# Low-rank factors in both halves of the partitions, multiplied in two rounded passes of 128 and 64 rows

## The chip, the core and the metric

One Trainium2 chip; the program runs on one of its cores. The metric is the device time in microseconds. Each time is one execution; of several the median is given.

## What is computed

A transformer block with adaptive layer norm. Only what bears on the change is shown: the second half is a mixture of eight experts, and the first two experts of the reference have low-rank additions to each of their three weight matrices.

```python
weights = _router_weights(x, Wr, temperature)
gate = jnp.einsum('btd,edf->ebtf', x, Wg)
up = jnp.einsum('btd,edf->ebtf', x, Wu)
gate = gate.at[:NL].add(jnp.einsum('btd,edr,erf->ebtf', x, Ga, Gb))
up = up.at[:NL].add(jnp.einsum('btd,edr,erf->ebtf', x, Ua, Ub))
mid = jax.nn.silu(gate) * up
out = jnp.einsum('ebtf,efd->ebtd', mid, Wd)
out = out.at[:NL].add(jnp.einsum('ebtf,efr,erd->ebtd', mid[:NL], Da, Db))
return jnp.einsum('bte,ebtd->btd', weights, out)
```

`NL` is 2, the rank `R` is 64, `D` and `F` are 256. The attention before it has 8 batches of 256 rows, 16 query heads and 4 key heads of 128.

## The kernel before

All instructions are written by hand for each engine, with semaphores between them; no scheduler moves anything. The order of the source is the order on the engine.

Attention runs in 64 slots, one for two heads of one batch: scores, tanh and exponential, the product with the values, the output projection, and beside these the projections of the next batch. Then come 32 tiles, each one expert on 512 rows (`TILES`, index `m`). A tile has two steps `up(g)`, each 24 matmuls of 512 columns into `ps_g` and `ps_u`, and two steps `down(d)`, each 12 matmuls of 256 columns. The first four tiles are spread over the last slots; from `m = NEXT = 4` on there is a loop over `m` on each engine.

Nearly every product is made of three passes over rounded data: an operand is stored as a rounded part (`hi`, type float32r) and the rest (`lo`), and `three` multiplies hi by hi, hi by lo and lo by hi. ScalarE rounds (`we_hi`, L1027), GpSimd subtracts (`we_lo`, L1660). Transposes, the router's logits, the product with the values (L663) and the low-rank products take plain float32.

Low-rank weights: rather than adding a product to every output, the kernel multiplies the two factors once, adds the 256x256 result to the expert's weight matrix while that still lies unrounded in `raw_e`, and lets the ordinary rounding follow. `low_rank(i)` (L754) has six calls, three matrices of each of two experts. Each multiplies two blocks of `lowA` by `lowB` into one PSUM bank, `ps_y` or `ps_turn` in turn. `fold(i)` on VectorE (L1331) adds the bank to `raw_e`. The two experts stand third and fourth in the kernel's order. The calls stand at the ends of four steps of the loop over the tiles, `LOW_STEPS`: two calls with m = 5, one with 6, one with 8, two with 9.

```python
LOW_STEPS = {NEXT + 1: [0, 1], NEXT + 2: [2], NEXT + 4: [3], NEXT + 5: [4, 5]}
...
                for k in range(KT):
                    mm = pe.matmul((ps_y[:], ps_turn[:, 0, :])[i % 2][:, k * F:(k + 1) * F], lowA[:, e, m3, k * P:(k + 1) * P],
                                   lowB[:, e, m3, :], start=(k == 0), stop=True, skip_group_check=True)
```

`lowA` and `lowB` take 64 partitions (the rank) by 2 x 3 x 256 elements. SP issues their loads (L521, L522) once the last output projection is done (`y_ready`), since they lie where the output weights were; behind them on the same queue stand the gate rows (`gates_b`, L523) and the remaining experts (`raw_e`, L505).

In step m = 4 ScalarE does the gate activations (`gate_of`, L1035), the normalised rows of the last batch, the rounding of `mid`, and `modulate2` for the last batch; in step m = 5 it rounds this batch (`h2_head`, L1011) between the two gate activations, and VectorE makes its low part `h2_lo` (L1323), which tile m = 6 is the first to read. GpSimd has `inv_std2` for the last batch, and then the low parts of the experts, from m = 6 on.

Of the kernel before, what the change touches and what calls it, by code (L numbers as in the profile page):

```python
# [13 lines left out]
P = 128  # L14
# [209 lines left out]
def build(nc, a, out):  # L224
# [16 lines left out]
    def sem(name):  # L241
        return ctx.enter_context(nc.semaphore(name))

    with ctx:
# [98 lines left out]
        r_eq = [place(f"r_eq{n}", [P, 4, NE, NE], F32, offset + 1024) for n, offset in enumerate((raw_at + 10240, h2f_at, probs_at + BLOCK))]  # L343
        part = place("part", [P, 2, TT, E], F32, k_at[1] + 4 * 4 * E)
        part_last = place("part_last", [P, 4, E], F32, k_at[1] + 4 * 4 * E + 4 * 2 * TT * E)
        lowA = place("lowA", [R, NL, 3, E], F32, wo_at)
        lowB = place("lowB", [R, NL, 3, E], F32, wo_at + 4 * NL * 3 * E)
        gates_b = place("gates_b", [P, B, E], F32, wo_at + 4 * H * E)

        raw_o = raw_e[:].rearrange("p a m f -> p (a m f)").rearrange("p (r k n) -> p r k n", r=RAW_RING, k=KT)  # L350
# [27 lines left out]
        cs_in = sem("cs_in")  # L378
        qks_in = sem("qks_in")
        low_in = sem("low_in")  # L380
        out_done = sem("out_done")
        silu_c = sem("silu_c")
        mod_cols = sem("mod_cols")
# [90 lines left out]
        def _(sp):  # L474
# [43 lines left out]
            sp.wait_ge(we_split, 1)  # L518
            expert(2)
            sp.wait_ge(y_ready, B)  # L520
            sp.dma_start(lowA[:], a["lowA"]).then_inc(low_in, 16)  # L521
            sp.dma_start(lowB[:], a["lowB"]).then_inc(low_in, 16)  # L522
            sp.dma_start(gates_b[:], gates_dram[:, E:2 * E].unsqueeze(0).broadcast_to([P, B, E])).then_inc(gates_b_in, 16)  # L523
            for e in range(3, NE):
                sp.wait_ge(we_split, 3 * (e - 1) - 2)
# [11 lines left out]
        def _(pe):  # L537
# [216 lines left out]
            def low_rank(i):  # L754

                e, m3 = divmod(i, 3)
                if i == 0:
                    pe.wait_ge(low_in, 32)
                    pe.wait_ge(x_updated, B)
                elif i == 1:  # L760
                    bank_free(len(TURN_LIST), 0)
                else:
                    pe.wait_ge(we_added, i - 1)
                for k in range(KT):
                    mm = pe.matmul((ps_y[:], ps_turn[:, 0, :])[i % 2][:, k * F:(k + 1) * F], lowA[:, e, m3, k * P:(k + 1) * P],
                                   lowB[:, e, m3, :], start=(k == 0), stop=True, skip_group_check=True)
                mm.then_inc(low_ready, 1)

            def slot(s):
# [85 lines left out]
        def _(act):  # L855
# [183 lines left out]
            def mid_head(g):  # L1039
# [3 lines left out]
                    act.wait_ge(down_ready, 2 * m - 2)  # L1043
                act.activation(mid_hi[:, m % 2, f, :], mid[:, f, :], ACT.Copy, scale=0.5 if g < SMOOTH else 1.0).then_inc(mid_hi_done, 1)  # L1044

            def route(g, stage):
                if stage == 0:
                    act.wait_ge(router, STEPS * g + 2)
                    act.activation(r_b[:], r_a[:], ACT.Exp, scale=-1.0).then_inc(router_act, 1)
                else:  # L1050
                    act.wait_ge(router, STEPS * g + 8)
                    act.activation(r_w[:], r_c[:], ACT.Exp, scale=-1.0 / 0.1).then_inc(router_act, 1)
                    act.activation(r_fb[:], r_c[:], ACT.Exp, scale=-1.0 / 0.3).then_inc(router_act, 1)
# [78 lines left out]
            for m in range(NEXT, len(TILES)):  # L1132
                gate_of(2 * m)
                if m in LATE_ROUTE_EXP:
                    route(LATE, LATE_ROUTE_EXP[m])
                if m == NEXT:
                    second_rows(B - 1)
                if m == NEXT + 1:
                    h2_head(B - 1)
                gate_of(2 * m + 1)  # L1140
                mid_head(2 * m)
                mid_head(2 * m + 1)
                if m == NEXT:
                    modulate2(B - 1)
                for e, m3 in EXPERT_STEPS.get(m, ()):
                    split_e(e, m3)

# [423 lines left out]
        def _(pool):  # L1571
# [149 lines left out]


            inv_std2(B - 1)
            for m in range(NEXT, len(TILES)):
                for e, m3 in EXPERT_STEPS.get(m, ()):
                    split_e(e, m3)
# [64 lines left out]
```

## Time and profile before

| what | value |
|---|---|
| median of 3 runs | 808.05 us (807.27 to 809.63) |
| the profiled execution | 808.01 us |
| its span | 806.3 us |
| TensorE busy | 795.3 us, 5116 matmul records |
| TensorE weight loads busy | 710.1 us |
| VectorE, ScalarE, GpSimd busy | 507.5, 462.2, 395.0 us |
| granted TensorE clock | full in all 40 slices |
| DMA | 21.53 MB, mean 27 GB/s |

The span is the time from the first to the last instruction that the profile has; the execution's own time has some 1.7 us more around it. A weight load is a record of its own (PEld) and runs beside matmuls (PE). The ends of matmuls are modelled, and overlap; what can be relied on is the distance from start to start. An unrounded float32 matmul is recorded as two.

### The profile page before, as it was taken

What the parts mean: (1) busy time and instruction counts of PE and PEld (TensorE: products, weight loads), DVE (VectorE), ACT (ScalarE), POOL (GpSimd) and SP (SyncE); (2) the same over time, 40 slices, a digit from 0 to 9 for tenths busy, and PEclk for the clock granted to TensorE, in tenths of its full rate; (3) what the DMA queues carried; (4) which work ended last, traced back from release to release, by engine and by line L of the source; (5) the groups of instructions that cost most, each with busy time, mean ns of one, the idle gap of its engine ahead of it and who ended that gap; (6) DMA issues with size and microseconds to landing.
All of it is one profiled execution on the core that took longest, in us unless ns stands there. A gap on an engine that the chain in (4) does not pass through costs nothing.

```text
span 806.3 us, 14755 instructions
## 1 busy us (share of the span) xinstructions
PE 795.3 (99%) x5116; PEld 710.1 (88%) x5116; DVE 507.5 (63%) x1074; ACT 462.2 (57%) x1255; POOL 395.0 (49%) x543
## 2 busy tenths in 40 slices
PE   9899999999999999999999999999999999999997
PEld 8688898999999999999999999899888888888887
DVE  5677676476476566557557658667785454454575
ACT  5777686677577677667767776643343232332322
POOL 3777587486576667567567656120011010110493
PEclk9999999999999999999999999999999999999999
DMA  9200010000000000000000000203010110100002
GB/s 333 103 28 2 1 61 1 1 8 2 0 8 2 1 7 2 2 2 6 1 1 8 1 2 2 79 1 94 38 40 2 40 40 1 40 0 1 1 1 105
DMA packets 8170, 21.53 MB, mean 27 GB/s; under 512 B 1561, under 2 KB 4249, under 8 KB 7969
## 3 DMA queue, kind: packets, MB, share of 16 engines
q1 hardware_dynamic: 7520, 20.51, 7.5%
q8 instruction: 42, 0.69, 0.4%
q14 instruction: 32, 0.25, 0.1%
q10 hardware_dynamic: 576, 0.08, 0.1%
HBM read 18.48 MB, written 2.11 MB: 26 GB/s over the span
## 4 chain that ended last, share of the span: by engine, by line
PE 93%; DVE 2%; POOL 1%; ACT 1%; issue 1%; DMA 1%; ACTq 0%; DVEq 0%; POOLq 0%
PE ps_o L663 14%; PE ps_proj L540 9%; PE ps_proj L542 9%; PE ps_proj L541 9%; PE ps_s L540 7%; PE ps_s L541 7%; PE ps_s L542 7%; PE ps_turn L592 4%; PE ps_y L540 4%; PE ps_y L541 4%; PE ps_y L542 4%; PE ps_turn L610 3%; PE ps_turn L540 2%; PE ps_turn L541 2%; PE ps_turn L542 2%; PE ps_o L542 2%
## 5 line engine op out<-in xcount | busy, mean ns | idle before, releaser
L663 PE MATMUL ps_o<-vaug,probs 128*128 128x129 f32 x1024 | 135.3, 275 | 1.6 <-POOL probs L1654 0.9
L663 PEld LDWEIGHTS ps_o<-vaug,probs 128*128 128x128 f32 x1024 | 129.1, 191 | 8.0 <-POOL probs L1654 1.4
L984 ACT ACTIVATE ps_s<-ps_s,knorm 128x512 f32<-128x512 f32 x128 | 79.1, 657 | 95.7 <-PE ps_s L542 95.5
L1267 DVE RECIPROCAL rden<-ps_o 128x2 f32<-128x2 f32 x128 | 21.8, 170 | 154.0 <-PE ps_o L663 153.9
L1660 POOL TENSOR_TENSOR we_lo<-raw_e,we_hi 128x512 fp32r<-128x512 f32 x22 | 28.4, 1316 | 182.3 <-ACT we_hi L1027 182.3
L1237 DVE TENSOR_TENSOR prod<-ps_proj,cs 128x1024 f32<-128x1024 f32 x76 | 92.5, 1217 | 10.9 <-ACT sq L927 10.9
L1605 POOL TENSOR_TENSOR root<-ssq,powers 128x4 f32<-128x4 f32 x76 | 77.7, 1023 | 27.6 <-ACT sq L927 27.6
L927 ACT ACTIVATE sq<-ps_proj 128x128 f32<-128x128 f32 x304 | 79.9, 278 | 18.2 <-PE ps_proj L542 15.2
L1621 POOL TENSOR_TENSOR prod<-prod 128x512 f32<-128x512 f32 x62 | 80.0, 1290 | 9.9 <-DVE prod L1237 9.9
L540 PE MATMUL ps_proj<-w_hi,h_hi 128*128 128x512 f32 x192 | 83.1, 433 | 0.9 <-DVE w_lo L1180 0.5
L1652 POOL TENSOR_SCALAR_AFFINE_SELECT probs<-probs 128x256 f32<-128x256 f32 x64 | 26.3, 410 | 106.1 <-ACT probs L992 105.8
L540 PE MATMUL ps_y<-wo_hi,oT_hi 128*128 128x256 f32 x256 | 75.8, 296 | 0.0
L542 PE MATMUL ps_proj<-w_hi,h_lo 128*128 128x512 f32 x192 | 75.7, 394 | 0.0
L541 PE MATMUL ps_proj<-w_lo,h_hi 128*128 128x512 f32 x192 | 75.4, 393 | 0.0
L1628 POOL TENSOR_TENSOR rows<-prod,rnorm 128x512 f32<-128x512 f32 x62 | 66.7, 1075 | 13.2 <-issue 4.7
L542 PE MATMUL ps_y<-wo_hi,oT_lo 128*128 128x256 f32 x256 | 71.4, 279 | 0.0
L541 PE MATMUL ps_y<-wo_lo,oT_hi 128*128 128x256 f32 x256 | 71.4, 279 | 0.0
L1044 ACT ACTIVATE mid_hi<-mid 128x512 fp32r<-128x512 f32 x64 | 40.2, 629 | 47.9 <-DVE mid L1352 26.0
L992 ACT ACTIVATE probs<-ps_s 128x1024 f32<-128x1024 f32 x64 | 66.2, 1035 | 0.0
L927 ACT ACTIVATION_READ_ACCUMULATOR sq<-ps_proj 128x1 f32 x304 | 63.4, 209 | 0.0
L1271 DVE TENSOR_TENSOR o_rows<-ps_o,rden 128x256 f32<-128x256 f32 x128 | 54.3, 424 | 4.4
L540 PE MATMUL ps_proj<-h_hi,we_hi 128*128 128x512 f32 x140 | 55.6, 397 | 0.0
(212 smaller groups left out, 2178.1 us busy)
## 6 DMA issues: line engine op xcount, KB each, us to landing
raw_e<-in_we SPq DMA_DIRECT2D x8, 768.0 KB, 4.3
raw_p<-in_wqkv SPq DMA_DIRECT2D x6, 512.0 KB, 8.1
raw_e<-in_wo SPq DMA_DIRECT2D x4, 512.0 KB, 11.6
x_all<-in_x SPq DMA_DIRECT2D x1, 1536.0 KB, 7.0
out<-acc SPq DMA_DIRECT2D x3, 512.0 KB, 2.6
x_all<-in_wmod SPq DMA_DIRECT2D x1, 1024.0 KB, 10.0
gates_a<-gate_rows_dram SPq DMA_DIRECT2D x8, 128.0 KB, 2.9
gates_b<-gate_rows_dram SPq DMA_DIRECT2D x1, 1024.0 KB, 8.0
```

What stands on the lines that cost most here:

```text
L540: pe.matmul(dst, hi, w_h, start=first, stop=False, skip_group_check=True)
L541: pe.matmul(dst, hi, w_l, start=False, stop=False, skip_group_check=True)
L542: return pe.matmul(dst, lo, w_h, start=False, stop=last, skip_group_check=True)
L663: mm = pe.matmul(ps_o[:, h * (D + 1):(h + 1) * (D + 1)], probs[:, s % 2, at:at + P], vaug[b % 2][:, k, i // 2, :], start=(h == 0 and k == ...
L927: squared = act.activation(sq[:, n % 2, h, :], ps_proj[:, u % 2, h * D:(h + 1) * D], ACT.Square, accum_out=ssq[:, n % 2, h:h + 1])
L984: act.activation(ps_s[:, t, :], ps_s[:, t, :], ACT.Tanh, scale=knorm[:, b % 2, t, i // 2:i // 2 + 1]).then_inc(tanh_done, 1)
L992: act.activation(probs[:, s % 2, :], ps_s[:].rearrange("p k n -> p (k n)"), ACT.Exp, scale=CAP).then_inc(exp_done, 1)
L1237: dve.tensor_tensor(prod[:, n % 2], src, cs[:, t].unsqueeze(2).broadcast_to([P, 2, 4, D]), ALU.mult).then_inc(rotated, 1)
L1271: dve.tensor_tensor(o_rows[:, t], o[:, :, 0:D], rden[:, t, :].unsqueeze(2).broadcast_to([P, 2, D]), ALU.mult).then_inc(o_rows_ready, 1)
L1605: pool.tensor_tensor(root[:, n % 2, :], ssq[:, n % 2, :], powers[:, 0:4], ALU.pow).then_inc(root_ready, 1)
L1621: pool.tensor_tensor(whole, whole, turned, ALU.add).then_inc(rot_sum, 1)
L1628: pool.tensor_tensor(rows[:, n % RING], prod[:, n % 2, 0], rnorm[:, n % 2, :].unsqueeze(2).broadcast_to([P, 4, D]), ALU.mult).then_inc(row ...
```

## The change

The factors are loaded twice, into partitions 0 to 63 and 64 to 127, by four DMAs. ScalarE rounds both over all 128 partitions, one expert in step m = 4 and one in step m = 5 (`low_round`). GpSimd then replaces, in partitions 64 to 127, the rounded `lowA_both` by the rest of it, and makes `lowB_lo` in partitions 0 to 63; this stands behind `inv_std2` and ahead of the experts' low parts. Each block product of `low_rank` becomes two passes over rounded data: one of 128 rows, `lowA_both` by `lowB_hi`, which gives hi by hi and lo by hi at once, and one of 64 rows, hi by lo. The product of lo by lo is left out.

```diff
-        lowA = place("lowA", [R, NL, 3, E], F32, wo_at)
-        lowB = place("lowB", [R, NL, 3, E], F32, wo_at + 4 * NL * 3 * E)
+        lowA = place("lowA", [P, NL, 3, E], F32, wo_at)
+        lowB = place("lowB", [P, NL, 3, E], F32, wo_at + 4 * NL * 3 * E)
+        lowA_both = place("lowA_both", [P, NL, 3, E], F32R, qT_at + 2 * 4 * 4 * E)
+        lowB_hi = place("lowB_hi", [P, NL, 3, E], F32R, wo_at + 4 * H * E + 4 * B * E)
+        lowB_lo = place("lowB_lo", [P, NL, 3, E], F32R, wo_at + 4 * NL * 3 * E)
...
-            sp.dma_start(lowA[:], a["lowA"]).then_inc(low_in, 16)
-            sp.dma_start(lowB[:], a["lowB"]).then_inc(low_in, 16)
+            for half in (slice(0, R), slice(R, P)):
+                sp.dma_start(lowA[half], a["lowA"]).then_inc(low_in, 16)
+                sp.dma_start(lowB[half], a["lowB"]).then_inc(low_in, 16)
...
                 if i == 0:
-                    pe.wait_ge(low_in, 32)
                     pe.wait_ge(x_updated, B)
                 elif i == 1:
                     bank_free(len(TURN_LIST), 0)
                 else:
                     pe.wait_ge(we_added, i - 1)
+                pe.wait_ge(low_split, 2 * e + 2)
                 for k in range(KT):
-                    mm = pe.matmul((ps_y[:], ps_turn[:, 0, :])[i % 2][:, k * F:(k + 1) * F], lowA[:, e, m3, k * P:(k + 1) * P],
-                                   lowB[:, e, m3, :], start=(k == 0), stop=True, skip_group_check=True)
+                    dst, at = (ps_y[:], ps_turn[:, 0, :])[i % 2][:, k * F:(k + 1) * F], slice(k * P, (k + 1) * P)
+                    pe.matmul(dst, lowA_both[:, e, m3, at], lowB_hi[:, e, m3, :], start=(k == 0), stop=False, skip_group_check=True)
+                    mm = pe.matmul(dst, lowA_both[0:R, e, m3, at], lowB_lo[0:R, e, m3, :], start=False, stop=True, skip_group_check=True)
                 mm.then_inc(low_ready, 1)
...
+            def low_round(e):
+                act.wait_ge(low_in, 64)
+                if e == 0:
+                    act.wait_ge(scores_ready, ALL)
+                    act.wait_ge(y_ready, B)
+                act.activation(lowA_both[:, e], lowA[:, e], ACT.Copy).then_inc(low_rounded, 1)
+                act.activation(lowB_hi[:, e], lowB[:, e], ACT.Copy).then_inc(low_rounded, 1)
...
                 if m == NEXT:
                     modulate2(B - 1)
+                    low_round(0)
+                if m == NEXT + 1:
+                    low_round(1)
...
             inv_std2(B - 1)
+            for e in range(NL):
+
+                pool.wait_ge(low_rounded, 2 * e + 2)
+                pool.tensor_tensor(lowA_both[R:P, e], lowA[R:P, e], lowA_both[R:P, e], ALU.subtract).then_inc(low_split, 1)
+                pool.wait_ge(low_split, 2 * e + 1)
+                pool.tensor_tensor(lowB_lo[0:R, e], lowB[0:R, e], lowB_hi[0:R, e], ALU.subtract).then_inc(low_split, 1)
+                pool.wait_ge(low_split, 2 * e + 2)
```

TensorE at the end of step m = 5, where calls 0 and 1 stand between the last pass of `down(9)` and the first of `up(12)`; before:

```order
L542 MATMUL ps_o<-we_hi_134,mid_lo 128x256
L765 MATMUL ps_y<-lowB,lowA 128x256 [waits x_updated,low_in]
L765 MATMUL ps_y<-lowB,lowA 128x256
L765 MATMUL ps_turn<-lowB,lowA 128x256 [waits logits_read]
L765 MATMUL ps_turn<-lowB,lowA 128x256
L540 MATMUL ps_s<-h_hi_128,we_hi_133 128x512 [waits mid_done,h2_split]
```

and with the change, where L774 is the pass of 128 rows and L775 the one of 64 (the size at a row's end is the output's), and L548 to L550 are the old L540 to L542:

```order
L550 MATMUL ps_o<-we_hi_134,mid_lo 128x256
L774 MATMUL ps_y<-lowB_hi,lowA_both 128x256 [waits low_split,x_updated]
L775 MATMUL ps_y<-lowB_lo,lowA_both 128x256
L774 MATMUL ps_y<-lowB_hi,lowA_both 128x256
L775 MATMUL ps_y<-lowB_lo,lowA_both 128x256
L774 MATMUL ps_turn<-lowB_hi,lowA_both 128x256 [waits low_split,logits_read]
L775 MATMUL ps_turn<-lowB_lo,lowA_both 128x256
L774 MATMUL ps_turn<-lowB_hi,lowA_both 128x256
L775 MATMUL ps_turn<-lowB_lo,lowA_both 128x256
L548 MATMUL ps_s<-h_hi_128,we_hi_133 128x512 [waits mid_done,h2_split]
```

Four matmuls became eight, and two kinds of them alternate. Nothing else on TensorE moved.

ScalarE with the change, from the end of step m = 4 to the first gate activation of step m = 6 (L1014 is `modulate2`, L1044 a gate activation, L1020 `h2_head`, L1053 the rounding of `mid`):

```order
L1014 ACTIVATE h2f_124<-ps_turn,modc 128x256
L1060 ACTIVATE lowA_both<-lowA 128x768 [waits y_ready,scores_ready,low_in]
L1061 ACTIVATE lowB_hi<-lowB 128x768
L1044 ACTIVATE silu<-ps_s 128x512 [waits mid_done,gu_ready]
L1020 ACTIVATE h_hi_128<-h2f_124 128x2x256 [waits proj_ready,h2_mod]
L1044 ACTIVATE silu<-ps_proj 128x512 [waits mid_done,gu_ready]
L1053 ACTIVATE mid_hi<-mid 128x512 [waits down_ready,mid_done] x2
L1060 ACTIVATE lowA_both<-lowA 128x768 [waits low_in]
L1061 ACTIVATE lowB_hi<-lowB 128x768
L1044 ACTIVATE silu<-ps_s 128x512 [waits mid_done,gu_ready]
```

The four rows L1060 and L1061 are new; the others follow each other before as they do here.

## Rows read from the trace of the kernel before

**Rows 1.** The page, busy time, share and instructions of TensorE and others.

```profile
PE 795.3 (99%) x5116; PEld 710.1 (88%) x5116; DVE 507.5 (63%) x1074; ACT 462.2 (57%) x1255; POOL 395.0 (49%) x543
```

**Rows 2.** The page, chain that ended last, shares by engine.

```profile
PE 93%; DVE 2%; POOL 1%; ACT 1%; issue 1%; DMA 1%; ACTq 0%; DVEq 0%; POOLq 0%
```

**Rows 3.** Timeline, TensorE, first pair: start us, us, engine, line, operation, rows*columns, output, count.

```profile
573.52 0.28 PE L541 MATMUL ps_o<-we_lo,mid_hi 128*128 128x256 f32 x1
573.64 0.28 PE L542 MATMUL ps_o<-we_hi,mid_lo 128*128 128x256 f32 x1
573.85 1.13 PE L765 MATMUL ps_y<-lowB,lowA 64*128 64x256 f32 x4
...
575.77 0.50 PE L540 MATMUL ps_s<-h_hi,we_hi 128*128 128x512 f32 x1
576.11 0.39 PE L541 MATMUL ps_s<-h_lo,we_hi 128*128 128x512 f32 x1
```

**Rows 4.** Timeline, TensorE, around the first single call.

```profile
584.21 0.28 PE L542 MATMUL ps_o<-we_hi,mid_lo 128*128 128x256 f32 x1
...
585.82 0.40 PE L541 MATMUL ps_s<-h_lo,we_hi 128*128 128x512 f32 x1
```

**Rows 5.** Timeline, weight loads, around the first pair; in brackets the idle time before.

```profile
573.53 0.19 PEld L542 LDWEIGHTS ps_o<-we_hi,mid_lo 128*128 128x128 f32 x1
573.85 0.73 PEld L765 LDWEIGHTS ps_y<-lowB,lowA 64*128 64x128 f32 x4
...
575.77 0.19 PEld L540 LDWEIGHTS ps_s<-h_hi,we_hi 128*128 128x128 f32 x1 [0.33 <-issue]
```

**Rows 6.** Timeline, TensorE, a slot of the attention; unrounded passes of 128 rows.

```profile
402.25 0.39 PE L542 MATMUL ps_proj<-w_hi,h_lo 128*128 128x512 f32 x1
402.48 1.05 PE L663 MATMUL ps_o<-vaug,probs 128*128 128x129 f32 x8
...
403.73 0.48 PE L540 MATMUL ps_proj<-w_hi,h_hi 128*128 128x512 f32 x1
404.04 0.40 PE L541 MATMUL ps_proj<-w_lo,h_hi 128*128 128x512 f32 x1
```

**Rows 7.** Timeline, weight loads, the same place.

```profile
402.25 1.09 PEld L663 LDWEIGHTS ps_o<-vaug,probs 128*128 128x128 f32 x8
```

**Rows 8.** Timeline, SP's queue: start and length of the issue.

```profile
555.90 0.51 SPq L521 DMA_DIRECT2D lowA<-in_lowA  x1
556.46 0.59 SPq L522 DMA_DIRECT2D lowB<-in_lowB  x1
...
557.73 101.87 SPq L505 DMA_DIRECT2D raw_e<-in_we  x4
```

**Rows 9.** DMA issues: output and source, count, KB each, us to landing.

```profile
lowA<-in_lowA SPq DMA_DIRECT2D x1, 384.0 KB, 4.6
lowB<-in_lowB SPq DMA_DIRECT2D x1, 384.0 KB, 5.8
```

**Rows 10.** Tile raw_e, 557 to 568 us, its one load.

```profile
DMA to landing us min/median/max: 9.2/9.2/9.2
```

**Rows 11.** Stretch 557 to 566: busy PE, PEld, DVE, ACT, POOL; clock, DMA share, GB/s.

```profile
557.00:566.00 9.00, 9.00 (x55) 8.00 (x54) 6.79 (x15) 4.24 (x8) 1.23 (x4) 1.00 1.01 284
```

**Rows 12.** Timeline, ScalarE, gate activations of steps m = 5 and 6.

```profile
566.06 0.60 ACT L1035 ACTIVATE silu<-ps_s 128x512 f32<-128x512 f32 x1 [0.39 <-PE ps_s L542]
...
569.71 0.60 ACT L1035 ACTIVATE silu<-ps_proj 128x512 f32<-128x512 f32 x1 [2.53 <-PE ps_proj L542]
...
577.47 0.60 ACT L1035 ACTIVATE silu<-ps_s 128x512 f32<-128x512 f32 x1 [4.30 <-PE ps_s L542]
```

**Rows 13.** Groups by line and shape: busy us, mean ns, idle before.

```profile
L874 ACT ACTIVATE w_hi<-raw_p 128x1024 fp32r<-128x1024 f32 x5 | 5.2, 1058 | 0.0
```

**Rows 14.** Timeline, GpSimd, low parts of an expert.

```profile
584.41 2.54 POOL L1660 TENSOR_TENSOR we_lo<-raw_e,we_hi 128x512 fp32r<-128x512 f32 x2 [23.42 <-ACT we_hi L1027]
```

**Rows 15.** Timeline, VectorE, low part of the last batch.

```profile
573.82 0.68 DVE L1323 TENSOR_TENSOR h_lo<-h2f,h_hi 128x512 fp32r<-128x512 f32 x1
```

More of the change, by code:

```diff
@@ L380, in build @@
         low_in = sem("low_in")
+        low_rounded = sem("low_rounded")
+        low_split = sem("low_split")
         out_done = sem("out_done")
```

## The prediction

> **What bounds the kernel now.** I read the page's busy shares first, then its chain of waits, then the low-rank stretches of the TensorE timeline beside the weight loads, and last the other engines and the DMA in the same 20 us. TensorE is busy for 795.3 of 806.3 us [rows 1], and the chain that ended last runs over it for 93% of the span [rows 2]: time is won or lost almost only by what TensorE issues, or by what it is made to wait for. The change touches four short places on TensorE: the low-rank products, 12 matmuls of 64 rows by 256 columns in six calls, two calls together at 573.9 us, one each at 584.4 and 602.6, two at 612.3. Each unrounded matmul stands in the trace as two records, so a call of two matmuls shows x4 [rows 3].
>
> **TensorE, before.** I take the distance between two ordinary matmul starts on either side of a group, less what these would have without the group (from a rounded 256-column pass to the next start it is 0.12 us [rows 3], from a rounded 512-column pass 0.23 [rows 6], together 0.35). For the first pair of calls: 576.11 - 573.64 = 2.47, less 0.35, is **2.12 us** [rows 3]. For a single call: 585.82 - 584.21 = 1.61, less 0.35, is **1.26 us** [rows 4]. The other single call and the other pair measure the same to 0.01. Sum: 2 x 2.12 + 2 x 1.26 = **6.76 us** of 806.
>
> **TensorE, after.** 12 unrounded matmuls become 24 rounded passes, each with 256 columns: 24 x 0.12 = **2.88 us** when such passes follow each other in one form [rows 3]. If that were all, 3.9 us would be saved. But the new passes alternate: 128 rows, 64 rows, 128, 64. The trace shows what a change of the number of rows costs. Going in, the pass after 573.64 starts 0.21 us later and not 0.12, and its weight load is at the same 573.85 us as itself; ordinarily the load starts 0.1 us ahead of its pass (load 573.53, pass 573.64) [rows 3, 5]. So 0.09 us of waiting, and about 0.1 us of a load that nothing covers. Coming out the same: the load at 575.77 stands beside its own pass, after 0.33 us in which no load ran, and the next pass follows after 0.34 us and not 0.23 [rows 3, 5, 6]. The size of both together: a pair has four records more than a single call and takes 2.12 - 1.26 = 0.86 us more, 0.215 each. Its 8 records are 1.72 us, and 2.12 - 1.72 = 0.40 us is left for two changes; a single call leaves 1.26 - 0.86 = 0.40 us too. So **0.20 us for each change of rows**, whatever the length of the group. That this is not the price of going from rounded to unrounded data is seen where unrounded 128-row passes follow a rounded one: the start comes 0.23 us after a 512-column pass, no later than ever, and its load starts 0.23 us ahead [rows 6, 7].
>
> A call now has four changes (into 64, back, into 64, back, since ordinary 128-row passes stand on both sides), where a whole group had two. 6 x 4 = 24 changes x 0.20 = 4.80 us. New total: 2.88 + 4.80 = 7.68 us against 6.76: **+0.9 us**. The work halves, and the changes take it back. Bounds of a change's price: 0 below (nothing in the trace lets a change gain), 0.33 above, the whole gap without a load [rows 5]. They give 2.88 us (-3.9) and 2.88 + 7.92 = 10.80 us (+4.0). I take 0.20, since it is measured on this shape of tile, in both directions together.
>
> The Trainium skill (TensorEngine Tiling (Array Packing), Key Properties) says that a change of the tiling mode drains TensorE, while a change of tile within a mode does not. By that rule alone all of the 24 changes pay, the cheaper cases among the rivals fall away, and the sum is +0.9 or more; the trace agrees at the eight changes that it has, but none of them has rounded data on both sides.
>
> **Transfers.** SP issues two more loads of 384 KB between the old two and the gate rows. The old ones landed at 555.90 + 4.6 = 560.5 and 556.46 + 5.8 = 562.3 us [rows 8, 9], the second 1.8 us behind the first. The DMA engines are full from 557 to 566 us [rows 11], so the two more come behind at the same pace: 562.3 + 2 x 1.8 = 565.9 us. The gate rows and the fourth expert move by 3.6 us; the expert landed at 557.73 + 9.2 = 566.9 [rows 8, 10], will land at 570.5, and is read by the fold behind the fourth call, at 602.6. They cost nothing.
>
> **ScalarE.** Four new roundings of 128x768. A 128x512 activation takes 0.60 us and a 128x1024 copy 1.06, so 0.85 each, two in a row 1.7 us [rows 12, 13]. The first two stand behind the modulation that ends at 565.7 (566.06 less 0.39 of idle time) [rows 12] and need the transfers of 565.9: they end at 567.6 and put the next gate activation back from 566.06 by 1.5 us. The one after that is at 569.7 (it waits 2.5 us for TensorE), and what the first feeds is wanted only with the next tile; the 1.5 us are covered. The only reader near is the last batch's h2_lo, done at 573.82 + 0.68 = 574.50 [rows 15], behind activations that come after 569.7, so it does not move; without that cover TensorE would wait in front of the ordinary pass at 575.77. The second two fall into the 4.30 us of idle time before 577.47 [rows 12]: nothing.
>
> **GpSimd.** Four new subtractions of 64x768. Two of 128x512 take 2.54 us, so 1.27 each [rows 14]; with 768 elements 1.9 us, and two one behind the other 3.8, plus 0.1 for the waits between. From 567.6 they end at **571.5 us**. TensorE wants them at 573.76: 2.3 us to spare. The other two end near 579, well before the fourth call, and before GpSimd's next work at 584.4, ahead of which it had been idle for 23 us [rows 14]. The wait put into each call is for a semaphore long raised; the old calls had such waits too, and inside a pair no time is seen there. Nothing.
>
> The sum: the profiled execution took 808.01 us, span 806.3 and 1.7 around it. 808.01 + 0.92 = 808.9; the median of the runs is 0.04 higher: **809.0 us**, +0.1%. A difference under 0.3% (2.4 us) is what I take as not told from no change in this kernel.
>
> **The rivals.**
> *Half the changes are free.* Unrounded passes before an ordinary one may be part of the price on the way back: after four 128-row transposes of unrounded data the first ordinary pass is also followed after 0.31 us and not 0.23 [rows 6], without any change of rows. If with rounded data only the way into 64 rows costs: 2.88 + 12 x 0.20 = 5.28, so -1.5 us: 806.6, still no change that can be told. Against it: the 0.09 us of waiting on the way back isn't explained so.
> *No change costs anything.* Loads go ahead of running passes whatever the rows, and what [rows 5] show comes from unrounded data of 64 rows only. Then -3.9 us: 804.2, faster. Against it speaks the way in, where the pass before is rounded and the load is still not ahead. The Trainium skill (TensorE: Matmul & The Clock Gate, the step-by-step section) says that a weight load is pulled ahead of running matmuls where it goes to the background buffer; taken alone, that rule would give this case, and the row at 573.85 is against it.
> *TensorE waits for the factors* (slower). If the four loads share the engines with the gate rows and the expert rather than going ahead of them, their last byte lands with the last of all, at 566.9 + 3.6 = 570.5 us. ScalarE then ends at 572.2, GpSimd at 576.1, and TensorE, there at 573.76, stands 2.3 us: 0.9 + 2.3 = +3.2, **811.3 us**. It decides from a landing at 568.2 us on (565.9 plus the 2.3 to spare). For it: the engines are full just then. Against it: lowB landed 4.6 us before the expert that was issued 1.3 us behind it [rows 8 to 10], so they do go in order.
> *A change is dearer than 0.20*, up to 0.33: up to +4.0, 812.1; slower by over 0.3% from 0.26 on.
>
> **How the numbers follow.** 0.20 for every change: 0.60. Half free: 0.15. All free: 0.10. A wait for the factors: 0.09. Dearer changes: 0.06, two thirds of them beyond 0.26. Faster by over 0.3%: 0.10. Slower: 0.09 + 0.04 = 0.13. Within: 0.77. The forecast is that of the likeliest case, 809.0. The range goes from 806.0, under the half-free case with a little for the spread of the runs, to 811.5, over the case with the wait; it leaves out the all-free case and the dearest changes, some 0.15.
>
> **What would show it.** In the TensorE timeline the four groups last 2.5, 1.3, 1.3 and 2.5 us by the same subtraction, with starts 0.3 us apart inside, and each weight load beside its own pass. If they last 1.0 and 0.5 the changes are free; 1.8 and 0.9 is the half-free case. Right about the rest are: the fourth transfer landed by 566, roundings near 0.85 us, the second subtraction over by 572, and no idle TensorE ahead of the first call. I am wrong if TensorE stands there, or if the starts inside a group are 0.12 apart.

## The result and the profile after

| | before | changed |
|---|---|---|
| median of 11 runs | 808.0 us (807.27 to 809.63) | 810.04 us (808.7 to 810.6) |
| profiled execution, span in it | 808.01, 806.3 us | 810.15, 808.4 us |
| mean granted clock of the profiled execution | 1.000 | 0.997 |

The changed kernel takes 1.002 times the time before (95% interval 1.0011 to 1.0029). The interval lies above 1, so in this comparison the changed kernel is a little slower, but by less than the 0.3% that the prediction named as its bound. It is 1.0 us above the 809.0 predicted. The page's first lines:

```profile
span 808.4 us, 14773 instructions
PE 797.5 (99%) x5116; PEld 711.5 (88%) x5116; DVE 508.5 (63%) x1074; ACT 465.8 (58%) x1259; POOL 403.3 (50%) x547
```

Against [rows 1] TensorE is busy 2.2 us longer, about as much as the span has grown by (2.1), and ScalarE and GpSimd have four instructions more each. The number of TensorE records is the same: 24 records of unrounded products went, 24 passes came.

The TensorE timeline at the first pair, which answers to [rows 3]:

```profile
575.11 0.28 PE L550 MATMUL ps_o<-we_hi,mid_lo 128*128 128x256 f32 x1
575.23 0.28 PE L774 MATMUL ps_y<-lowB_hi,lowA_both 128*128 128x256 f32 x1
575.44 0.38 PE L775 MATMUL ps_y<-lowB_lo,lowA_both 64*128 64x256 f32 x1
575.75 0.38 PE L774 MATMUL ps_y<-lowB_hi,lowA_both 128*128 128x256 f32 x1
576.07 0.38 PE L775 MATMUL ps_y<-lowB_lo,lowA_both 64*128 64x256 f32 x1
...
577.63 0.50 PE L548 MATMUL ps_s<-h_hi,we_hi 128*128 128x512 f32 x1
577.97 0.39 PE L549 MATMUL ps_s<-h_lo,we_hi 128*128 128x512 f32 x1
```

The first low-rank pass starts 0.12 us behind the ordinary one. From there on the starts are 0.31 apart, since each changes the number of rows: 0.12 and about 0.19 for the change, going to 64 rows (575.23 to 575.44 is 0.21) and coming back. The group is 577.97 - 575.11 - 0.35 = 2.51 us, where it was 2.12. The single call, by its own two rows:

```profile
586.08 0.28 PE L550 MATMUL ps_o<-we_hi,mid_lo 128*128 128x256 f32 x1
...
587.69 0.40 PE L549 MATMUL ps_s<-h_lo,we_hi 128*128 128x512 f32 x1
```

1.61 - 0.35 = 1.26 us, as in [rows 4] before. The other pair measures 2.51 again and the other single call 1.25. Sum 7.53 us against 6.76: +0.78 by the unrounded differences. The weight loads of the same place, which answer to [rows 5]:

```profile
575.11 0.19 PEld L774 LDWEIGHTS ps_y<-lowB_hi,lowA_both 128*128 128x128 f32 x1
575.44 0.18 PEld L775 LDWEIGHTS ps_y<-lowB_lo,lowA_both 64*128 64x128 f32 x1
575.75 0.19 PEld L774 LDWEIGHTS ps_y<-lowB_hi,lowA_both 128*128 128x128 f32 x1
```

The load for 575.23 is there 0.12 us ahead of its pass; those for 575.44 and 575.75 start with their passes, and nothing covers them.

**But 0.78 is not 2.2.** SP issues the first factor load 1.47 us later than before [rows 8], before anything of the change has run:

```profile
557.37 0.51 SPq L529 DMA_DIRECT2D lowA<-in_lowA  x1
```

So 1.47 us come from elsewhere, and only 0.71 behind this place (the first pass of the last down product starts at 795.85 before and 798.03 now, 2.18 later; 2.18 - 1.47 = 0.71). The stretches of 42 to 46 us show what it is (busy time and count of PE, PEld, DVE, ACT, POOL, then granted clock, DMA share, GB/s). Before:

```profile
42.00:44.00 2.00, 2.00 (x16) 1.82 (x16) 1.50 (x1) 1.28 (x3) 0.42 (x1) 1.00 0.03 8
44.00:46.00 2.00, 2.00 (x14) 1.74 (x13) 1.19 (x3) 1.95 (x7) 0.54 (x2) 1.00 0.00 0
```

Changed:

```profile
42.00:44.00 2.00, 2.00 (x9) 1.58 (x8) 1.82 (x4) 0.48 (x1) 0.78 (x1) 0.58 0.03 8
44.00:46.00 2.00, 2.00 (x11) 1.99 (x10) 0.00 (x0) 2.00 (x4) 0.00 (x0) 0.56 0.00 0
```

A clock of 0.58 and 0.56 means mostly half clock (1.2 of 2.4 GHz). The program is the same there in both kernels, and so is what TensorE did just before. In the changed kernel, and in the kernel before:

```profile
41.37 0.50 PE L548 MATMUL ps_s<-qT_hi,kT_hi 128*128 128x512 f32 x1 [2.15 <-DVE qT_lo L1282]
```

```profile
41.02 0.50 PE L540 MATMUL ps_s<-qT_hi,kT_hi 128*128 128x512 f32 x1 [2.15 <-DVE qT_lo L1262]
```

Both stood 2.15 us for the low part of the queries; in one the clock fell 1 us after work had resumed, in the other it did not. Of the 1.47 us, 0.35 lie ahead of this place (41.37 against 41.02), and 1.1 behind it. The 0.35 is within what profiles differ by: in the nine that have this wait the start lies between 41.02 and 41.49. The runs below tell whether the change has a part in the 1.1.

The support work of the change, ScalarE and GpSimd:

```profile
567.32 0.85 ACT L1060 ACTIVATE lowA_both<-lowA 128x768 fp32r<-128x768 f32 x1 [0.16 <-DMA lowB<-in_lowB]
568.07 0.83 ACT L1061 ACTIVATE lowB_hi<-lowB 128x768 fp32r<-128x768 f32 x1
568.81 0.58 ACT L1044 ACTIVATE silu<-ps_s 128x512 f32<-128x512 f32 x1
```

```profile
568.98 1.84 POOL L1747 TENSOR_TENSOR lowA_both<-lowA,lowA_both 64x768 fp32r<-64x768 f32 x1 [6.51 <-ACT lowB_hi L1061]
570.90 1.84 POOL L1749 TENSOR_TENSOR lowB_lo<-lowB,lowB_hi 64x768 fp32r<-64x768 f32 x1
```

Less the 1.47 us: the last factor landed at 565.8, the roundings took 0.85 and 0.83, and the second subtraction ended at 571.27. TensorE came 575.23 - 572.74 = 2.5 us after it and waited for nothing.

### The profile page after: what moved, and what is told of

It reads as the page before. It is cut to its first block, busy times and chain, and to the rows that moved or that the text cites. A ratio compares the mean times of both kernels' runs of the same rounds, so it can differ in the third digit from the quotient of the medians.

```text
span 808.4 us, 14773 instructions
## 1 busy us (share of the span) xinstructions
PE 797.5 (99%) x5116; PEld 711.5 (88%) x5116; DVE 508.5 (63%) x1074; ACT 465.8 (58%) x1259; POOL 403.3 (50%) x547
## 4 chain that ended last, share of the span: by engine, by line
PE 94%; DVE 1%; ACT 1%; POOL 1%; issue 1%; DMA 1%; ACTq 0%; DVEq 0%; POOLq 0%
PE ps_o L671 14%; PE ps_proj L548 9%; PE ps_proj L550 9%; PE ps_proj L549 9%; PE ps_s L548 7%; PE ps_s L549 7%; PE ps_s L550 7%; PE ps_turn L600 4%; PE ps_y L548 4%; PE ps_y L550 4%; PE ps_y L549 4%; PE ps_turn L618 3%; PE ps_turn L548 2%; PE ps_turn L549 2%; PE ps_turn L550 2%; PE ps_o L550 2%
## 5 line engine op out<-in xcount | busy, mean ns | idle before, releaser
L548 PE MATMUL ps_proj<-w_hi,h_hi 128*128 128x512 f32 x192 | 83.1, 433 | 0.4 <-DVE h_lo L1204 0.4
L548 PE MATMUL ps_y<-wo_hi,oT_hi 128*128 128x256 f32 x256 | 75.8, 296 | 0.0
L550 PE MATMUL ps_proj<-w_hi,h_lo 128*128 128x512 f32 x192 | 75.7, 394 | 0.0
L550 PE MATMUL ps_y<-wo_hi,oT_lo 128*128 128x256 f32 x256 | 71.5, 279 | 0.0
L1053 ACT ACTIVATE mid_hi<-mid 128x512 fp32r<-128x512 f32 x64 | 40.2, 628 | 47.9 <-DVE mid L1372 26.0
L548 PE MATMUL ps_proj<-h_hi,we_hi 128*128 128x512 f32 x140 | 55.6, 397 | 0.0
```

Of the source, the lines that this page charges most:

```text
L548: pe.matmul(dst, hi, w_h, start=first, stop=False, skip_group_check=True)
L550: return pe.matmul(dst, lo, w_h, start=False, stop=last, skip_group_check=True)
```

## The experiments

Each comparison has its own runs of the kernel before, on the same chip. Since about half of all executions have a mean granted clock under 0.999, I give beside the median the median of the executions at 0.999 or more, called **full-clock** ones here. This takes stretches of half clock out of both sides, wherever they lie; their place is seen only in the profiled executions.

**Both passes of 128 rows.** Does the price hang on the change of rows, or on the rounded passes as such? In this kernel and those built on it the second pass adds a product that the changed kernel leaves out (low part of A times low part of B); all else is computed alike.

```
-  mm = pe.matmul(dst, lowA_both[0:R, e, m3, at], lowB_lo[0:R, e, m3, :], ...)
+  mm = pe.matmul(dst, lowA_both[:, e, m3, at], lowB_lo[:, e, m3, :], ...)
-  pool.tensor_tensor(lowB_lo[0:R, e], lowB[0:R, e], lowB_hi[0:R, e], ALU.subtract)
+  pool.tensor_tensor(lowB_lo[:, e], lowB[:, e], lowB_hi[:, e], ALU.subtract)
```

> The second pass takes 128 rows too: lowB_lo is made over all partitions, so the pass adds lo by lo as well, and TensorE has no change of rows left. Theory 1 (each change of rows costs 0.195 us, as the four groups of the changed kernel show, and nothing else in the change costs): 24 passes at 0.12 us are 2.88 us against 6.76 before, so 3.9 us less than the kernel before, about 804.1 us, ratio 0.995; the four groups last 0.96, 0.48, 0.48, 0.96 us, with starts 0.12 apart. Tile m = 6 may wait up to 0.2 us for h2_lo. Rival A (a low-rank pass costs 0.31 us whatever its rows, because its operands alternate): the groups stay at 2.5 and 1.3 us and the time at 0.8 us over before. Rival B (what costs beyond the groups is the support work, 0.8 us): 3.1 us less than before, 804.9.

Measured: 805.67 us (804.6 to 805.81, 5 runs) against 808.41; ratio 0.9959 (0.9947 to 0.9972). Full-clock: 804.65 against 808.25, -3.6. The TensorE timeline:

```profile
573.92 0.28 PE L775 MATMUL ps_y<-lowB_lo,lowA_both 128*128 128x256 f32 x1
...
574.16 0.28 PE L775 MATMUL ps_y<-lowB_lo,lowA_both 128*128 128x256 f32 x1
574.67 0.38 PE L774 MATMUL ps_turn<-lowB_hi,lowA_both 128*128 128x256 f32 x1 [0.24 <-DVE r_log L1337]
574.89 0.28 PE L775 MATMUL ps_turn<-lowB_lo,lowA_both 128*128 128x256 f32 x1
```

From 573.92 to 574.16 are two steps of 0.12 us: with equal rows the passes cost what the 24 x 0.12 of the prediction says. The price is the change's alone. Something new is seen too: the second call now comes so early that it waits for VectorE to read the router's logits out of the bank it writes. That costs 574.89 - 574.16 - 0.24 = 0.49 us, and -3.9 + 0.5 = -3.4 is close to the -3.6 measured.

**Same passes, grouped.** All passes as in the changed kernel, but a call runs 128, 128, 64, 64 rows: two changes a call, four rounded passes.

```
+  for lo in range(2):
       for k in range(KT):
+          if lo == 0: pe.matmul(dst, lowA_both[:, e, m3, at], lowB_hi[:, e, m3, :], ...)
+          else: mm = pe.matmul(dst, lowA_both[0:R, e, m3, at], lowB_lo[0:R, e, m3, :], ...)
```

> As the changed kernel, but each call does its two passes of 128 rows first and then its two of 64: two changes of rows for each call and not four, 12 in all. Theory 1: 2.88 + 12 x 0.195 = 5.22 us against 6.76 before, 1.5 us less than before, 806.5; a pair of calls lasts 0.96 + 0.78 = 1.74 us, a single call 0.87; start to start 0.12 between passes of the same rows and 0.31 at a change. Rival A (it is the pass that is dear, not the change): 2.5 and 1.3 us as in the changed kernel, +0.8. Half-free case (only the way into 64 rows costs, about 0.2, and the way back nothing): a pair lasts 0.96 + 0.4 = 1.36 us.

Measured: 806.96 us, ratio 0.9983 (0.9974 to 0.9992); full-clock 806.74 against 808.25, -1.5. The single call:

```profile
584.51 0.28 PE L550 MATMUL ps_o<-we_hi,mid_lo 128*128 128x256 f32 x1
584.63 0.40 PE L776 MATMUL ps_y<-lowB_hi,lowA_both 128*128 128x256 f32 x2
584.97 0.50 PE L778 MATMUL ps_y<-lowB_lo,lowA_both 64*128 64x256 f32 x2
...
585.73 0.40 PE L549 MATMUL ps_s<-h_lo,we_hi 128*128 128x512 f32 x1
```

585.73 - 584.51 - 0.35 = 0.87 us: four passes at 0.12 and 0.39 for two changes. With half the changes gone half their price is gone. The pair is 1.83, of which 0.1 is the second call's wait for the logits.

**Three passes of 64 rows.** One load of each factor into 64 partitions, low parts of both, three rounded passes of 64 rows for each product: more passes than the change has, but two changes for a group.

```
-  pe.matmul(dst, lowA_both[:, e, m3, at], lowB_hi[:, e, m3, :], ...)
+  pe.matmul(dst, lowA_both[0:R, e, m3, at], lowB_hi[0:R, e, m3, :], ...)
+  pe.matmul(dst, lowA_lo[0:R, e, m3, at], lowB_hi[0:R, e, m3, :], ...)
   mm = pe.matmul(dst, lowA_both[0:R, e, m3, at], lowB_lo[0:R, e, m3, :], ...)
```

> The factors are loaded once, into 64 partitions, and each block product is three rounded passes of 64 rows (hi by hi, lo by hi, hi by lo), so a group has two changes of rows as before the change, now between rounded data. Theory 1: 36 passes x 0.12 = 4.32 us plus 8 changes x 0.195 = 1.56, together 5.88 us against 6.76: 0.9 us less than before, 807.1; a pair lasts 1.44 + 0.39 = 1.83 us, a single call 0.72 + 0.39 = 1.11. Rival A (a rounded pass of 64 rows is dear in itself, 0.31 us): 36 x 0.31 = 11.2 us, 4.4 us over before, 812.4.

Measured: 807.3 us, ratio 0.9984 (0.9976 to 0.9993); full-clock 807.23 against 808.25, -1.0. The single call:

```profile
584.23 0.28 PE L551 MATMUL ps_o<-we_hi,mid_lo 128*128 128x256 f32 x1
584.44 0.38 PE L775 MATMUL ps_y<-lowB_hi,lowA_both 64*128 64x256 f32 x1
584.66 0.28 PE L776 MATMUL ps_y<-lowB_hi,lowA_lo 64*128 64x256 f32 x1
...
585.14 0.28 PE L777 MATMUL ps_y<-lowB_lo,lowA_both 64*128 64x256 f32 x1
585.35 0.50 PE L549 MATMUL ps_s<-h_hi,we_hi 128*128 128x512 f32 x1
585.68 0.40 PE L550 MATMUL ps_s<-h_lo,we_hi 128*128 128x512 f32 x1
```

1.45 - 0.35 = 1.10 us, six passes at 0.12 and 0.38 for two changes. 36 passes beat 24, because they change 8 times and not 24. Here the two directions can be told apart, since passes of 64 rows stand between them. Going in, the starts are 0.21 and then 0.22 apart, where 0.12 and 0.12 are ordinary: 0.19 us. Coming back they are 0.21 and 0.33 apart, where 0.12 and 0.23 are ordinary: 0.20 us.

**The support work alone.** All four loads, the roundings, the subtractions and the wait, but the products stay the old unrounded ones, read from the factors as loaded (one low part goes to a place of its own, so that they stay whole; what is rounded is not used).

```
-  pe.matmul(dst, lowA_both[:, e, m3, at], lowB_hi[:, e, m3, :], ...)
-  mm = pe.matmul(dst, lowA_both[0:R, e, m3, at], lowB_lo[0:R, e, m3, :], ...)
+  mm = pe.matmul(dst, lowA[0:R, e, m3, at], lowB[0:R, e, m3, :], ...)
```

> Everything of the change but its passes: four loads, four roundings, four subtractions and the wait for them on TensorE, while the products stay the 12 unrounded matmuls of 64 rows of the kernel before (they read partitions 0 to 63 of the raw factors; one low part goes to a place of its own). Theory 1: the groups last 2.12 and 1.26 us as before and the time is that of before, within 0.1 us, 808.0. Rival B (the support work costs the 0.8 us that the measured difference of 1.6 us has beyond the groups' 0.8): 808.8, ratio 1.001, with lost time outside of the four groups and, if it is a wait, idle TensorE ahead of the first call.

Measured: 809.07 us, ratio 1.0007 (0.9998 to 1.0016); full-clock 808.13 against 808.25. The pair:

```profile
573.65 0.28 PE L550 MATMUL ps_o<-we_hi,mid_lo 128*128 128x256 f32 x1
573.86 1.13 PE L773 MATMUL ps_y<-lowB,lowA 64*128 64x256 f32 x4
...
576.11 0.39 PE L549 MATMUL ps_s<-h_lo,we_hi 128*128 128x512 f32 x1
```

Start, length and end agree with [rows 3] to 0.01 us. Loads, roundings and subtractions cost nothing that shows.

**The changed kernel again.** How often is the mean clock under 0.999, with the change and without?

> The changed kernel itself once more, beside the two below, to compare executions with and without a stretch of half clock near 43 us. Theory 1 (the groups alone cost: 8 changes more... 24 changes x 0.195 + 2.88 = 7.56 us against 6.76 before): executions whose mean granted clock is 0.999 or 1.000 lie 0.8 us over those of the kernel before with the same clock, 809.0 against 808.25 on the last chip; those at 0.995 to 0.998 are 1 to 2 us longer in both kernels. Rival C (the change itself makes the clock fall at 43 us): clearly more than the third to half of executions that fall before, and the medians apart by 1.5 us or more.

Measured: 809.1 us against 809.06, ratio 1.0005 (0.9996 to 1.0014). Full-clock: 808.86 (5 of 11) against 808.0 (6 of 16), +0.87; in the first comparison 808.87 (4 of 11). Over the four comparisons of the experiments the kernel before had a clock under 0.999 in 44 of 79 executions, the changed one in its two comparisons in 13 of 22. So it comes about as often, as far as 22 executions can tell. For the share of the first result beyond +0.9 the lower clock is then the likely cause, but that is argued and not shown: the clocks of that comparison's eleven executions of the kernel before are not on record (three of them lie above 809.2 us).

**The factors issued late.** The prediction's slower rival, made real: SP issues the gate rows and the fourth expert ahead of the factors.

```
   sp.wait_ge(y_ready, B)
+  sp.dma_start(gates_b[:], ...)
+  sp.wait_ge(we_split, 4)
+  expert(3)
   for half in (slice(0, R), slice(R, P)):
...
-  sp.dma_start(gates_b[:], ...)
-  for e in range(3, NE):
+  for e in range(4, NE):
```

> As the changed kernel, but SP issues the gate rows and the fourth expert ahead of the four factor loads, so that these land last. The loads ahead took 2.8 and 1.8 us of full engines, so the fourth factor load lands 4.6 us later, near 570.5 us where the kernel before has its times. Theory 1 with the prediction's arithmetic: rounding to 572.2, subtractions to 576.0, TensorE there at 573.8 stands 2.2 to 2.3 us ahead of the first call, so 2.3 us over the changed kernel: 811.3. If there is more cover than reckoned, under 1 us of idle TensorE; if the gate activation behind the roundings carries on to later steps, more than 3 us.

Measured: 817.1 us (815.62 to 819.12, 4 runs), ratio 1.0106 (1.0089 to 1.0122): 8.0 above the changed kernel, far more than the 2.3 expected. ScalarE's first rounding:

```profile
571.92 0.84 ACT L1062 ACTIVATE lowA_both<-lowA 128x768 fp32r<-128x768 f32 x1 [6.19 <-DMA lowB<-in_lowB]
```

TensorE:

```profile
577.42 0.35 PE L776 MATMUL ps_y<-lowB_hi,lowA_both 128*128 128x256 f32 x1 [3.44 <-POOL lowB_lo L1751]
...
579.17 0.58 PE L776 MATMUL ps_turn<-lowB_hi,lowA_both 128*128 128x256 f32 x1 [0.46 <-DVE r_log L1339]
...
582.23 0.63 PE L552 MATMUL ps_s<-h_hi,we_lo 128*128 128x512 f32 x1
```

And the stretches, columns as above:

```profile
578.00:580.00 2.00, 1.54 (x5) 0.94 (x4) 2.00 (x6) 0.94 (x2) 0.91 (x1) 0.65 0.00 0
580.00:584.00 4.00, 4.00 (x10) 2.78 (x10) 2.69 (x6) 0.00 (x0) 2.72 (x2) 0.50 0.01 4
584.00:588.00 4.00, 4.00 (x16) 3.21 (x15) 1.66 (x4) 1.11 (x3) 0.00 (x0) 0.82 0.00 0
```

The last factor landed 1.4 us later than the 570.5 reckoned with, so the wait is 3.44 us and not 2.3. Then comes what I had left out: after the wait the clock falls to half for 2 x 0.35/0.5 + 4 + 4 x 0.18/0.5 = 6.8 us, half of which is lost, 3.4. A 512-column pass takes 0.63 us there and 0.39 at full clock. With the second call's 0.46: 3.4 + 3.4 + 0.5 = 7.3 us. That is a little too much, since part of the 0.46 lies within the time counted as half clock; the trace itself gives 6.9 us over the changed kernel (see the last table of this section). The profiled execution, 815.62 us at a mean clock of 0.996, is the shortest of the four. The others are longer the lower their clock: 816.78 at 0.994, 817.43 at 0.992, 819.12 at 0.990.

**Both of 128 rows, logits read earlier.** Takes away the new wait of the first experiment.

```
   product(2 * m)
+  if m == NEXT + 1:
+      h2_tail(B - 1)
+      read_logits(B - 1)
...
-  if m == NEXT + 1:
-      h2_tail(B - 1)
-      read_logits(B - 1)
```

> As all128, and VectorE makes the last batch's h2_lo and reads its logits right behind the first product of step m = 5 (idle until 571 us there) and not behind the second tile half. In all128 TensorE stood 0.24 us ahead of call 1 for that read. Theory 1: no wait ahead of call 1, the first pair of calls lasts 0.96 us, and the time is 0.3 us under all128: 4.0 us under the kernel before at the same clock. If another wait takes its place, it shows as idle TensorE ahead of tile m = 6 and the time stays that of all128.

Measured: 805.82 us (6 runs), ratio 0.9964 (0.9952 to 0.9977). The wait is gone: the second call's first pass starts 0.12 us behind the last of the first call. The time doesn't show the 0.4 us: 5 of the 6 executions had a clock under 0.999, and the one without took 804.47 us against 808.0 for the kernel before, -3.5, where it was -3.6 without the earlier reading. The trace shows why so little is left:

```profile
598.89 0.36 PE L548 MATMUL ps_turn<-we_hi,mid_hi 128*128 128x256 f32 x1 [0.16 <-DVE acc L1410]
```

The first pair of calls is 0.51 us shorter than in the kernel without the earlier reading, but 24 us behind it TensorE now waits for VectorE to read another bank (`acc`), which gives 0.30 us back. 0.2 us remain.

**The idle time filled.** TensorE multiplies the identity by itself, 15 times, where it stands for the queries at 39 us; nothing reads the result. In the kernel before, in the changed one, and in the last one.

```
   def scores(s):
+      if s == 2:
+          pe.wait_ge(exp_done, s)
+          for _ in range(15):
+              pe.matmul(ps_s[:, 1, 0:P], ident[:], ident[:], start=True, stop=True, ...)
```

> The kernel before, with 15 unused 128x128 products of the identity put where TensorE stands 2.1 us near 40 us for the first two qT_lo of the third slot (written to the scores' bank, which the scores clear). Theory (the half clock at 40 to 46 us follows from that idle time, and falls or not by chance): no execution has the half clock there, the mean granted clock is 0.999 or 1.000 in nearly all, and the median comes down to that of the undisturbed executions of the kernel before, 808.0 to 808.3, 1 us under its own median on this chip. Rival (the fall has another cause, or the idle time earlier counts): about half of the executions still at 0.995 to 0.998 and a median near 809.

> The changed kernel with the same filling. If the half clock goes with the idle time, what is left between this and the filled kernel before is the groups' 0.8 us alone: a median of 808.8 to 809.0 against 808.0 to 808.3. If the change brings more than the groups, they stay 1.5 us or more apart.

> all128_early with the same filling. Theory: 4.0 us under the filled kernel before, a median of 804.1 to 804.5, about 4.5 us under the median of the kernel before, ratio 0.9945. If the filling delays the scores (its products run beyond the arrival of qT_lo), it shows as less than that by up to 0.3 us.

In the order of the three: 809.13, 809.8 and 805.72 us; ratios 0.9998 (0.9989 to 1.0007), 1.0011 (1.0002 to 1.002) and 0.9958 (0.9944 to 0.9971). Full clock in 10 of 11, 9 of 11 and 4 of 5 executions: with the idle time filled, the lower clock is nearly gone in all three. The changed kernel then stands 0.67 us above the kernel before, both filled. But the filler was too long. From the filled kernel before:

```profile
39.55 3.51 PE L639 MATMUL ps_s<-ident 128*128 128x128 f32 x30
42.83 0.48 PE L540 MATMUL ps_s<-qT_hi,kT_hi 128*128 128x512 f32 x1
```

The 15 products are 30 records of about 0.11 us, where I had taken 15; the scores no longer wait, they come 1.8 us later than at 41.02. What the clock gave, the filler took.

**Eight products.** The same with `range(8)`, in the kernel before and in the last one (both passes of 128 rows, logits read earlier).

> The kernel before with 8 products in the gap and not 15. The 15 showed as 30 records of 0.107 us, 3.2 us in a gap of 2.1, and cost the 1 us that they should have saved; 8 are 1.7 us and end before qT_lo arrives. Theory: no half clock at 42 to 46 us, the scores of the third slot start when they do without the filling, and the median is 808.0 to 808.3. Rival (0.4 us of idle time is enough, or the half clock has another cause): still near half of the executions at 0.998 or less.

> all128_early with 8 products in the gap. Theory: 4.0 us under before_filled8, a median of 804.1 to 804.5, ratio to the kernel before 0.994 to 0.995.

Measured: the kernel before with it 808.35 us (808.04 to 809.53), ratio 0.9993 (0.9984 to 1.0002), against 808.46. So the filling by itself gives nothing that can be told from the medians; what it takes away are the long executions, 9 of the 15 unfilled ones being under 0.999 and only 1 of the 11 filled ones. The last one **804.63 us** (804.46 to 804.94, 5 runs), ratio 0.9946 (0.9934 to 0.9959): the fastest version, 3.7 us under the filled kernel before, and all five executions at full clock. Its fillers leave a short wait:

```profile
39.18 1.95 PE L647 MATMUL ps_s<-ident 128*128 128x128 f32 x16
41.49 0.50 PE L548 MATMUL ps_s<-qT_hi,kT_hi 128*128 128x512 f32 x1 [0.36 <-DVE qT_lo L1286]
```

One of the eleven executions of the filled kernel before still had half clock, the profiled one, and at another place:

```profile
10.00:15.00 5.00, 5.00 (x27) 4.70 (x26) 3.62 (x4) 3.43 (x6) 0.00 (x0) 0.70 1.03 418
```

**One stretch in every profile.** The half clock near 43 us lies ahead of all low-rank calls, so a stretch that begins behind it measures the edits without it. I take the distance from the last ordinary pass ahead of the first call (573.64 before, 575.11 changed) to the first pass of the last down product (795.85 and 798.03). Except in the kernel with late factors the granted clock is 1.00 throughout it.

| kernel, profiles | the stretch, us | against before |
|---|---|---|
| before, three (two of them filled) | 222.19 to 222.21 | |
| changed, three (one filled) | 222.92 to 222.93 | +0.71 |
| the support work alone | 222.20 | 0.0 |
| same passes, grouped | 220.78 | -1.43 |
| three passes of 64 rows | 221.30 | -0.91 |
| both passes of 128 rows | 218.77 | -3.44 |
| the same, logits read earlier, three (two filled) | 218.57 to 218.58 | -3.63 |
| the factors issued late | 229.81 | +7.60, 6.89 over changed |

Profiles of one kernel agree to 0.02 us here, so these differences are the edits' own.

## Why the prediction was right, and where it was not

- **What bounds the kernel.** TensorE does: each experiment on its passes moved the time by what its timeline says (-3.6, -1.5 and -1.0 us in full-clock executions, -3.4, -1.4 and -0.9 in the stretch).
- **The price of a change of rows**, 0.20 us, was the step that carried the forecast. Measured: (2.51 - 8 x 0.12)/8 = 0.194 in the pair. It is the same into 64 rows and back (0.19 and 0.20 by the rows of the three-pass kernel), and the same for rounded and unrounded data. Taking it from unrounded passes of this tile was sound.
- **The sum on TensorE**, +0.92: +0.78 in the groups, +0.71 in the stretch that holds all of them, +0.87 in full-clock executions of one comparison, +0.67 between the filled kernels. The parts were 24 x 0.12 and 24 x 0.20; a little of the second was too much.
- **The median**, +2.0 us in the first comparison: the part above +0.9 goes with the lower clock, which 7 of that comparison's 11 executions of the changed kernel had. In the profiled one it is the half clock near 43 us; where the other six had it, and how many of the kernel before's, is not on record. I had read the clock of 1.00 in the profiled execution before as the kernel's own, though its runs reached from 807.27 to 809.63, so that a second level was there to be suspected. The step that set the profiled execution level with the median added the term to a full-clock execution, while the changed kernel's median fell among those with the lower clock. The forecast foresaw nothing of this: that 809.0 is 1.0 us off and not more is no merit of it, and the right part is the +0.9.
- **Transfers, roundings, subtractions**: landing 565.9 forecast, 565.8 measured after the shift; 0.85 against 0.85 and 0.83; 1.9 against 1.84; 571.5 against 571.27; 2.3 to spare against 2.5. "Nothing" is what the support work costs by its own experiment. The gate activation came 1.3 us later, as it should (1.5), and nobody waited.
- **Half the changes free** fell by the grouped kernel: in full-clock executions the changed kernel stands 0.87 above the kernel before and the grouped one 1.5 below, 2.4 us for 12 changes taken away, 0.20 each (2.14 us and 0.18 each in the stretch, where a new wait of 0.1 us stands against it); were only the way in paid, it would be 6 x 0.20 = 1.2. **All free** fell by the starts 0.31 apart; where the rows don't change it is what happens. The rule that weight loads are pulled ahead, if the row groups don't conflict or the load goes to the background buffer (Trainium skill, TensorE: Matmul & The Clock Gate, the step-by-step section), holds in the rows shown where the number of rows stays, with the load 0.12 us ahead of its pass (575.11 and 575.23), and not at a change of rows (575.44 and 575.44). The rule that a change of the tiling mode drains TensorE (Trainium skill, TensorEngine Tiling (Array Packing), Key Properties) agrees with all 24, where the load starts with its own pass and 0.19 us is paid; that the engine drains is not itself seen in a row.
- **TensorE waits for the factors** did not happen, as the order on the queue said, but its price was wrong: 2.3 us for the wait, where the late load costs 6.9 us in the profiled execution and 8.0 in the median. What failed in this rival is that I took a wait of TensorE at its length alone: the wait was 3.44 us, and half clock followed it.

## What to carry to other kernels

Where short matmuls stand among others, count how often neighbouring passes differ in their number of rows: here each difference costs 0.19 us, more than a rounded 256-column pass (0.12), so that 36 passes with 8 changes beat 24 with 24, and 24 of full height beat both, though they compute a term nobody needs. When a stretch gets shorter, look which reader holds the buffer it writes next. And before a difference of a few tenths of a per cent is given to an edit, sort the executions of both kernels by granted clock, and compare one stretch of the traces that holds the whole edit and nothing of the disturbance: here it gave 0.71 us three times over, where the medians gave 2.0, 0.04 and 0.67.

## What the runs showed of the hardware that was not expected

- **Half clock after a short idle time, by chance.** Nine of the profiles have a wait of 2.13 to 2.15 us of TensorE near 39 to 41 us. In three of them (the changed kernel twice, both passes of 128 rows with the logits read earlier once) the granted clock falls to half within about 1.2 us of the work's resuming (0.58 and 0.56 over 42 to 46 us in the first of them); in the other six it stays full. By the two traces above it costs 1.1 us. Of executions without a profile only the mean clock is known: without the change it was under 0.999 in 44 of 79, and in each of the four comparisons the median of these is 1.1 to 1.3 us above that of the full-clock ones. In the five kernels with that time filled, 5 of 43 executions have a clock under 0.999. The 3.44 us wait of the late factors was followed by 6.8 us at half clock in its profile. Why one execution has it and another, with the same idle time, has not, stays open.
- **VectorE held up by GpSimd.** A small operation of VectorE takes 0.24 us in the kernel before, where GpSimd is idle:

```profile
577.45 0.24 DVE L1416 TENSOR_SCALAR r_a<-r_log,r_s 128x32 f32<-128x32 f32 x1
```

With both passes of 128 rows and the logits read earlier it takes 1.83 us. VectorE, and then GpSimd with one of the new subtractions:

```profile
577.79 1.83 DVE L1436 TENSOR_SCALAR r_a<-r_log,r_s 128x32 f32<-128x32 f32 x1
```

```profile
577.74 1.84 POOL L1749 TENSOR_TENSOR lowB_lo<-lowB,lowB_hi 128x768 fp32r<-128x768 f32 x1
```

It ends at 579.62, GpSimd at 579.58. In the changed kernel it takes 1.11 us and also ends 0.04 behind GpSimd. It goes the other way too: in the same profile a subtraction takes 2.31 us, beside VectorE's `h_lo` (570.29 to 570.97), which keeps its 0.68 us:

```profile
570.37 2.31 POOL L1749 TENSOR_TENSOR lowB_lo<-lowB,lowB_hi 128x768 fp32r<-128x768 f32 x1
```

The Trainium skill (SBUF — State Buffer, the section on two separate sides) says that a GpSimd operation and a VectorE operation that uses two ports, or reads two SBUF operands, hold a pair of ports exclusively for the whole instruction, so that the other blocks. The trace agrees with such a block, though no run isolates it, and no row shows in which mode the small operation ran. The other VectorE operations beside the subtractions, the folds that read PSUM among them (0.68 us), kept their times, and TensorE waited for none of it here.
